# Expert weights of 64 steps copied into a ring of three places, with expert, split buffer and state columns taken from registers

## The chip, the cores and the metric

The kernel runs on one core of one Trainium2 chip. The metric is the device time of one launch in microseconds (us); lower is better.

## The reference

Input x is 16 sequences of 256 rows with 128 channels (4096 rows). It is normalised, and two branches are computed from the normalised rows xn. All data are float32.

```python
xn = layernorm(x)
# branch 1: a gated recurrence over time, per channel
state = state * d_t + u_t ; mixed = r_t * state
s = (groupnorm(mixed) * gn_w + gn_b) * g @ W_out.T + b_out
# branch 2: R = 4 rounds, each over E = 4 experts, top 2 of 4 by a router
cur = xn
for r in range(4):
    logits = cur @ Wg[r] + bg[r]
    cw = softmax over the two largest logits, zero elsewhere
    hmid = gelu(cur @ W1[e] + b1[e])                  # 128 -> 512
    cur = cur + sum_e cw[:, e] * (hmid @ W2[e] + b2[e])   # 512 -> 128
out = x + s * silu(cur)
```

## The kernel before

**Tiling.** The 4096 rows are kept transposed (channels on the partitions) in `cur`, as 8 blocks of 512 columns. A turn is one block in one round, so there are 32 turns; turn k works on block k % 8 in round k // 8. A turn has 4 steps, one for each expert, so there are 128 steps; step s is expert s % 4 of turn s // 4.

**Numbers.** Each fp32 operand is split into a high and a low part of type fp32r, and a product is three matmuls: high by high, low weight by high, high weight by low. The weights of all four experts stay in on-chip memory for the whole kernel, in `w1_hi`, `w1_lo`, `w2_hi`, `w2_lo`. The split of a turn's block is in one of five buffers of `cur_hi` and `cur_lo` (buffer k % 5).

**A step.** `up(s)` on TensorE is 12 matmuls (3 for each of the 4 hidden tiles, lines 1079, 1080, 1083) into `h_bank`. ScalarE applies GELU (L465, output `g`) and makes the high part `g_hi` (L471); VectorE makes the low part `g_lo` (L759). `down(s)` on TensorE is 12 matmuls (L1140, L1142, L1152) into `y_bank`. VectorE combines it with bias and gate into `tmp` (L773, `combine`), and GpSimd issues a DMA that adds `tmp` to the block's columns of `cur` (L415), one in flight at a time. TensorE's order is written out by hand: in iteration s it does `up(s + 1)`, then `down(s)`, then, in some iterations, the router's logits, then in 7 iterations of every 14, beginning at 15, one projection of the recurrent branch (`project`, three matmuls into `p_bank`). `mixers_at` says which: the stage is (s - 15) mod 14, and stages 0, 1, 2, 3, 5, 6 and 12 have a projection, as long as blocks are left.

**Gates.** The router's gates are made for four turns at once. For turns 8 to 11, 12 to 15, 16 to 19 and 20 to 23 VectorE writes them to `cw` (L752) in its iterations 30, 46, 62 and 78. For each turn k, `spread_gates(k)` on SyncE issues a small write of the gates to DRAM (`cw_scratch<-cw`, L312, 8 KB), then waits until it has landed (`cw_saved`), and then issues the read that spreads them over all partitions (`cw_b<-cw_scratch`, L321, 1024 KB). The write waits for `cw_ready` and for `combined` (2 + 4 (k - 1)), which stands for the combine of step 4k - 5. SyncE runs its DMAs in program order, and all its transfers go to one queue (queue 1 of the profile). From turn 4 to 24 SyncE has nothing else to do than `spread_gates`.

**Semaphores that matter here.** `up_done` counts the four hidden tiles of every step, `down_done` the steps whose down is finished, `gelu_done` the GELU tiles, `summed` the landed additions.

Of the kernel before, what the change touches and what calls it, by code (L numbers as in the profile page):

```python
# [5 lines left out]
D = 128  # L6
# [4 lines left out]
BLK = 512  # L11
# [80 lines left out]
def mixer_gated_experts(nc, x, proj_t, mixes, wout_t, chan_vecs, wg, bg, w1, b1, w2, b2, cw_scratch, out):  # L92
# [7 lines left out]
    with ExitStack() as ctx:  # L100
        def sb(name, shape, dt=f32):
            return ctx.enter_context(nc.sbuf_tensor(name, shape, dt))
# [4 lines left out]
        def sem(name):  # L107
            return ctx.enter_context(nc.semaphore(name))
# [3 lines left out]

        cur = sb("cur", [128, TOK])

        w1_hi, w1_lo = sb("w1_hi", [128, E, F], f32r), sb("w1_lo", [128, E, F], f32r)
        w2_hi, w2_lo = sb("w2_hi", [128, E * FT, D], f32r), sb("w2_lo", [128, E * FT, D], f32r)
# [9 lines left out]
        gnw4, gnb2 = sb("gnw4", [128, 1]), sb("gnb2", [128, 1])  # L126
        mix = sb("mix", [128, 6])
        ident = sb("ident", [128, 128])
        warm = sb("warm", [128, 1])

        cur_hi, cur_lo = sb("cur_hi", [128, SPLITS, BLK], f32r), sb("cur_lo", [128, SPLITS, BLK], f32r)
        g = sb("g", [128, 2, FT * BLK])
        g_hi, g_lo = sb("g_hi", [128, 2, FT * BLK], f32r), sb("g_lo", [128, 2, FT * BLK], f32r)
        tmp = sb("tmp", [128, SUMS, BLK])
        cw_b = sb("cw_b", [128, 2, BLK * E])

# [68 lines left out]
        g_lo_done = sem("g_lo_done")  # L205
        down_done = sem("down_done")
        combined = sem("combined")
        r_full, r_empty = sem("r_full"), sem("r_empty")
        p_full, p_empty = sem("p_full"), sem("p_empty")
        lgd_ready, lgth_ready = sem("lgd_ready"), sem("lgth_ready")  # L210
# [15 lines left out]

        def as_f32(ap):
            return ap.bitcast(f32)

        GATEW, SMALL, MIXW = 2, 3, 2  # L230

# [25 lines left out]
        def _(sp):  # L257
# [112 lines left out]
            spread_gates(3)  # L370
            for b in range(4, NB):
                copy_block(b)
            END_TURN = END_FROM // E
            for k in range(4, END_TURN):
                spread_gates(k)
            load_x_again(0)
            load_x_again(1)
# [15 lines left out]
        @block.gpsimd  # L393
        def _(pool):
            pool.memset(ident[:, :], 0.0).then_inc(made, 1)
            pool.memset(ahead[:, :, :, :], 0.0).then_inc(made, 1)
            pool.wait_ge(made, 2)
            pool.affine_select(out=ident[:, :], in_=ident[:, :], compare_op=ALU.not_equal, fill=1.0,
                               base=0, pattern=[[-1, 128]], channel_multiplier=1).then_inc(made, 1)
            pool.memset(cw_e[:, :, :], 0.0).then_inc(gates_padded, 1)  # L400
            pool.memset(xn_t[:, :, 0:1], 0.0).then_inc(edge_zeroed, 1)

            for s in range(STEPS - ADDED_BY_DVE):
                for b in at_step(STORE_BEFORE, s):
# [10 lines left out]
                pool.dma_start(cur[:, block_of(s // E)], tmp[:, s % SUMS, :], accum_op=ALU.add).then_inc(summed, DMA)  # L415

        @block.scalar
        def _(act):
# [8 lines left out]

            def high_w2(e):
                act.wait_ge(w2_loaded[e], DMA)
                nc.scalar.activation(w2_hi[:, e * FT:(e + 1) * FT, :], w2_raw[e], ACT.Copy).then_inc(w2_high, 1)  # L430

            def high_mixw():
                act.wait_ge(mixw_loaded, DMA * MIXW)
# [131 lines left out]
        def _(dve):  # L565
# [71 lines left out]
                                        ALU.subtract).then_inc(w1_low, 1)  # L637

            def low_w2(e):
                h = slice(e * FT, (e + 1) * FT)  # L640
                dve.wait_ge(w2_high, e + 1)
                nc.vector.tensor_tensor(w2_lo[:, h, :], w2_raw[e], as_f32(w2_hi[:, h, :]),
                                        ALU.subtract).then_inc(w2_low, 1)

            def low_mixw():
# [431 lines left out]
        def _(pe):  # L1077
# [4 lines left out]
            def mm_low(out_ap, w_hi, v_lo):  # L1082
                return nc.tensor.matmul(out_ap, w_hi, v_lo, start=False, stop=True)  # L1083

            def turn_normed(b):
# [21 lines left out]
            def up(s1):  # L1107

                k, e = s1 // E, s1 % E
                q = k % SPLITS  # L1110
                if k == 0:
                    pe.wait_ge(w1_low, e + 2 if e > 0 else 1)
                if s1 == 0:
                    pe.wait_ge(first_high, 1)
                if e == 0:
                    pe.wait_ge(cur_split, 2 * k + 1)
                for ft in range(FT):
                    if s1 == 0 and ft == 1:
                        pe.wait_ge(w1_low, 2)
                    if s1 > 0:  # L1120
                        pe.wait_ge(gelu_done, FT * (s1 - 1) + ft + 1)
                    w = slice(ft * D, (ft + 1) * D)
                    mm_high(hb[ft][:, :], w1_hi[:, e, w], w1_lo[:, e, w], cur_hi[:, q, :])
                    if e == 0 and ft == 0:
                        pe.wait_ge(cur_split, 2 * (k + 1))
                    mm_low(hb[ft][:, :], w1_hi[:, e, w], cur_lo[:, q, :]).then_inc(up_done, 1)

            def down(s):

                e, b = s % E, s % 2  # L1130
                if s < E:
                    pe.wait_ge(w2_high, e + 1)
                pe.wait_ge(combined, s + 1)
                if s == 0:
                    pe.wait_ge(p_empty, 1)
                for ft in range(FT):
                    if ft % 2 == 0:
                        pe.wait_ge(g_hi_done, 2 * s + ft // 2 + 1)
                    hi = g_hi[:, b, ft * BLK:(ft + 1) * BLK]
                    nc.tensor.matmul(yb[b][:, :], w2_hi[:, e * FT + ft, :], hi, start=(ft == 0), stop=False)  # L1140
                    if s >= E:
                        nc.tensor.matmul(yb[b][:, :], w2_lo[:, e * FT + ft, :], hi, start=False, stop=False)  # L1142
                if s < E:

                    pe.wait_ge(w2_low, e + 1)
                    for ft in range(FT):
                        nc.tensor.matmul(yb[b][:, :], w2_lo[:, e * FT + ft, :], g_hi[:, b, ft * BLK:(ft + 1) * BLK],
                                         start=False, stop=False)
                for ft in range(FT):
                    if ft % 2 == 0:  # L1150
                        pe.wait_ge(g_lo_done, 2 * s + ft // 2 + 1)
                    last = nc.tensor.matmul(yb[b][:, :], w2_hi[:, e * FT + ft, :], g_lo[:, b, ft * BLK:(ft + 1) * BLK],  # L1152
                                            start=False, stop=(ft == FT - 1))
                last.then_inc(down_done, 1)

            def down_halves(s, sums, done):

                e, b = s % E, s % 2
                pe.wait_ge(combined, s + 1)
                for n in range(2):  # L1160
                    if n == 0 and s == STEPS - 1:
# [3 lines left out]
                    for ft in range(FT):  # L1165
                        if n == 0 and ft % 2 == 0:
                            pe.wait_ge(g_hi_done, 2 * s + ft // 2 + 1)
                        hi = g_hi[:, b, ft * BLK + n * HALF:ft * BLK + (n + 1) * HALF]
                        nc.tensor.matmul(sums[n][:, 0:HALF], w2_hi[:, e * FT + ft, :], hi, start=(ft == 0), stop=False)
                        nc.tensor.matmul(sums[n][:, 0:HALF], w2_lo[:, e * FT + ft, :], hi, start=False, stop=False)  # L1170
                    for ft in range(FT):
                        if n == 0 and ft % 2 == 0:
                            pe.wait_ge(g_lo_done, 2 * s + ft // 2 + 1)
                        lo = g_lo[:, b, ft * BLK + n * HALF:ft * BLK + (n + 1) * HALF]
                        last = nc.tensor.matmul(sums[n][:, 0:HALF], w2_hi[:, e * FT + ft, :], lo, start=False, stop=(ft == FT - 1))
                    last.then_inc(done, 1)

            def logits(n):
# [102 lines left out]
```

## Time and profile before

| what | value |
|---|---|
| time, median of 2 runs (784.88 and 784.97) | 784.92 us |
| span of the profiled execution, first to last instruction | 782.9 us |
| its own time, which is among the two | 784.9 us, 2.0 more than the span |
| TensorE busy | 777.2 us, 99% |
| VectorE busy | 689.3 us, 88% |
| ScalarE busy | 641.1 us, 82% |
| GpSimd busy | 115.2 us, 15% |
| DMA, mean over the span | 81.62 MB, 104 GB/s |
| granted TensorE clock | 1.00 throughout |

The engines are named PE (TensorE matmul), PEld (its weight loads, which run beside the matmuls), DVE (VectorE), ACT (ScalarE), POOL (GpSimd) and SPq (SyncE issuing a DMA). A matmul's row gives the time at which it starts and a modelled length of 0.39 us; back to back they start every 0.23 us. A DMA is issued by an engine's queue, and "to landing" is the time from the start of its issue until its semaphore has been counted up.

### The profile page before, as it was taken

Reading aid. Unit: us, or ns where it says so; the run is one execution under the profiler, and the core shown is the slowest. Engines: PE = TensorE matmul, PEld = TensorE weight load, DVE = VectorE, ACT = ScalarE, POOL = GpSimd, SP = SyncE. Lnnn points to the kernel's source line nnn. Section 1 sums busy time; section 2 is a strip of 40 time slices with the busy share of each in tenths; the row PEclk is TensorE's granted clock in tenths of the full one; section 3 lists DMA queues with packets and bytes.
Section 4 is the critical chain, followed back from the end, with each engine's and each line's share of the span. In section 5 each row is a group of like instructions: output and inputs, shape, how many; then the busy total and the mean of one; then the engine's idle time right before and its main releaser. Section 6 shows DMA issues by size and latency. Waiting matters only on the chain.

```text
span 782.9 us, 9951 instructions
## 1 busy us (share of the span) xinstructions
PE 777.2 (99%) x3392; PEld 619.2 (79%) x3392; DVE 689.3 (88%) x1096; ACT 641.1 (82%) x873; POOL 115.2 (15%) x141
## 2 busy tenths in 40 slices
PE   8999999999999999999999999999999999999998
PEld 6778788887888878888788887888877788888887
DVE  7999987899888889879899788987988989988998
ACT  7989888787888877888788877887877878888886
POOL 0122111111111111111111111111111111111110
PEclk9999999999999999999999999999999999999999
DMA  8467572332642416333154322643227434655453
GB/s 267 139 132 182 128 208 50 95 95 41 148 89 62 107 28 163 92 64 88 33 157 107 81 57 41 149 108 96 41 41 175 108 56 107 134 123 122 70 117 71
DMA packets 77010, 81.62 MB, mean 104 GB/s; under 512 B 48800, under 2 KB 54688, under 8 KB 72992
## 3 DMA queue, kind: packets, MB, share of 16 engines
q0 software_dynamic: 18624, 34.61, 25.8%
q1 hardware_dynamic: 57920, 46.11, 19.5%
q8 instruction: 27, 0.44, 0.2%
q10 hardware_dynamic: 416, 0.26, 0.1%
q14 instruction: 23, 0.19, 0.1%
HBM read 41.91 MB, written 3.93 MB: 59 GB/s over the span
## 4 chain that ended last, share of the span: by engine, by line
PE 95%; ACT 2%; DVE 2%; issue 0%; DMA 0%; DVEq 0%
PE h_bank L1079 15%; PE h_bank L1080 15%; PE h_bank L1083 15%; PE y_bank L1152 15%; PE y_bank L1142 15%; PE y_bank L1140 14%; PE p_bank L1079 2%; PE p_bank L1083 2%; PE p_bank L1080 2%; PE r_bank L1189 1%; ACT g L465 1%; ACT g_hi L471 1%; DVE g_lo L759 0%; DMA cur<-in_x 0%; DVE stats L600 0%
## 5 line engine op out<-in xcount | busy, mean ns | idle before, releaser
L465 ACT ACTIVATE g<-h_bank,b_c 128x512 f32<-128x512 f32 x512 | 329.3, 682 | 77.8 <-PE h_bank L1083 77.0
L759 DVE TENSOR_TENSOR g_lo<-g,g_hi 128x1024 fp32r<-128x1024 f32 x256 | 310.0, 1222 | 72.8 <-ACT g_hi L471 71.2
L471 ACT ACTIVATE g_hi<-g 128x1024 fp32r<-128x1024 f32 x256 | 271.8, 1062 | 8.1
L415 POOL DMA_DIRECT2D cur<-tmp x126 | 110.6, 878 | 642.4 <-DVE tmp L773 544.1
L1079 PE MATMUL h_bank<-cur_hi,w_hi 128*128 128x512 f32 x512 | 202.9, 396 | 0.2 <-ACT cur_hi L513 0.2
L1083 PE MATMUL h_bank<-cur_lo,w_hi 128*128 128x512 f32 x512 | 202.2, 395 | 0.0
L1080 PE MATMUL h_bank<-cur_hi,w_lo 128*128 128x512 f32 x512 | 202.1, 395 | 0.0
L1140 PE MATMUL y_bank<-g_hi,w_hi 128*128 128x512 f32 x504 | 196.2, 393 | 0.0
L1142 PE MATMUL y_bank<-g_hi,w_lo 128*128 128x512 f32 x488 | 193.6, 397 | 0.0
L1152 PE MATMUL y_bank<-g_lo,w_hi 128*128 128x512 f32 x504 | 137.9, 395 | 0.1
L1079 PEld LDWEIGHTS h_bank<-cur_hi,w_hi 128*128 128x128 f32 x512 | 96.2, 188 | 26.6 <-issue 3.8
L1083 PEld LDWEIGHTS h_bank<-cur_lo,w_hi 128*128 128x128 f32 x512 | 96.2, 188 | 23.3 <-DVE cur_lo L663 0.2
L1080 PEld LDWEIGHTS h_bank<-cur_hi,w_lo 128*128 128x128 f32 x512 | 96.3, 188 | 22.6
L1152 PEld LDWEIGHTS y_bank<-g_lo,w_hi 128*128 128x128 f32 x504 | 94.6, 188 | 23.1 <-DVE g_lo L759 0.5
L1140 PEld LDWEIGHTS y_bank<-g_hi,w_hi 128*128 128x128 f32 x504 | 94.7, 188 | 22.4 <-issue 0.8
L1142 PEld LDWEIGHTS y_bank<-g_hi,w_lo 128*128 128x128 f32 x488 | 91.7, 188 | 23.0
L773 DVE SCALAR_TENSOR_TENSOR tmp<-y_bank,b_c,cw_b 128x512 f32<-128x512 f32 x126 | 93.6, 743 | 0.0
L836 DVE SCALAR_TENSOR_TENSOR xm<-xx,mix,xn_t 128x512 f32<-128x512 f32 x48 | 35.7, 744 | 0.3
L824 DVE TENSOR_TENSOR part_lo<-xm,part_hi 128x512 fp32r<-128x512 f32 x48 | 33.2, 692 | 1.7
L708 DVE TENSOR_TENSOR cur_lo<-cur,cur_hi 128x512 fp32r<-128x512 f32 x31 | 21.5, 692 | 1.1
L822 DVE TENSOR_SCALAR part_hi<-xm 128x512 fp32r<-128x512 f32 x48 | 20.8, 434 | 1.6
L1079 PE MATMUL p_bank<-part_hi,pj_hi 128*128 128x512 f32 x48 | 19.3, 401 | 0.0
(153 smaller groups left out, 410.5 us busy)
## 6 DMA issues: line engine op xcount, KB each, us to landing
cur<-tmp POOLq DMA_DIRECT2D x126, 256.0 KB, 3.3
cw_b<-cw_scratch SPq DMA_DIRECT2D x31, 1024.0 KB, 5.2
xn_t<-cur SPq DMA_DIRECT2D x8, 256.0 KB, 3.1
cur<-in_x SPq DMA_DIRECT2D x7, 256.0 KB, 5.0
xr<-in_x SPq DMA_DIRECT2D x28, 64.0 KB, 3.4
out<-o SPq DMA_DIRECT2D x28, 64.0 KB, 2.1
xn_scratch<-o POOLq DMA_DIRECT2D x6, 256.0 KB, 3.0
xr<-xn_scratch SPq DMA_DIRECT2D x24, 64.0 KB, 2.5
```

Of the source, the lines that this page charges most:

```text
L415: pool.dma_start(cur[:, block_of(s // E)], tmp[:, s % SUMS, :], accum_op=ALU.add).then_inc(summed, DMA)
L465: nc.scalar.activation(g[:, gb, ft * BLK:(ft + 1) * BLK], hb[ft][:, :], ACT.Gelu_apprx_tanh, bias=b1_c[:, e * FT + ft:e * FT + ft + 1]).th ...
L471: nc.scalar.activation(g_hi[:, gb, h], g[:, gb, h], ACT.Copy).then_inc(g_hi_done, 1)
L759: nc.vector.tensor_tensor(g_lo[:, gb, h], g[:, gb, h], as_f32(g_hi[:, gb, h]), ALU.subtract).then_inc(g_lo_done, 1)
L773: nc.vector.scalar_tensor_tensor(out=tmp[:, s % SUMS, :], in0=yb[s % 2][:, :], scalar=b2_c[:, e:e + 1], in1=cw_b[:, q, e * BLK:(e + 1) * BLK],
L836: link(nc.vector.scalar_tensor_tensor(out=xm[:, :, :], in0=xx[:, :, :], scalar=mix[:, k:k + 1], in1=xs[:, :, 1:LEN + 1], op0=ALU.mult, op1 ...
L1079: nc.tensor.matmul(out_ap, w_hi, v_hi, start=True, stop=False)
L1080: nc.tensor.matmul(out_ap, w_lo, v_hi, start=False, stop=False)
L1083: return nc.tensor.matmul(out_ap, w_hi, v_lo, start=False, stop=True)
L1140: nc.tensor.matmul(yb[b][:, :], w2_hi[:, e * FT + ft, :], hi, start=(ft == 0), stop=False)
L1142: nc.tensor.matmul(yb[b][:, :], w2_lo[:, e * FT + ft, :], hi, start=False, stop=False)
L1152: last = nc.tensor.matmul(yb[b][:, :], w2_hi[:, e * FT + ft, :], g_lo[:, b, ft * BLK:(ft + 1) * BLK], start=False, stop=(ft == FT - 1))
```

## The change

1. **Ring.** The weights are laid out so that high and low part of one expert are next to each other (`w1_all`, `w2_all`: 2 x 512 elements, 4 KB per partition and expert). A new tile `staged` has three places of 512 KB. For steps 32 to 95 (64 of the 128), TensorE takes its weights from `staged`, not from the resident tiles. SyncE copies them there from on-chip memory: 128 DMAs of 512 KB, one for the up weights and one for the down weights of each step. Units are numbered in the order in which TensorE uses them: up 32, up 33, down 32, up 34, down 33, ... Unit v goes to place v % 3, and from v = 3 on its DMA waits until unit v - 3 has been used (`up_done` or `down_done`).
2. **Waits.** `up(s)` and `down(s)` wait for `stage_full` of their place before their first matmul in these steps.
3. **Order on SyncE.** `stage_step(s)` for the four steps 4(k - 1) to 4k - 1 stands ahead of `spread_gates(k)`. It issues the unit up(s + 1) and the unit down(s) (at s = 32 also up(32)).
4. **Registers.** A table of small numbers is made once by three GpSimd iotas. SyncE loads 4 registers from it (the expert, source of the copy), TensorE 16 registers before `up(24)` (the split buffer of a turn), and GpSimd 16 before its step 24 (the block for the addition). In steps 32 to 95 the 12 moving operands of `up`, the copies and the additions are addressed through them.
5. **Room.** `g_lo` lies in the same bytes as `g`, so that the low part is written over its input.

```diff
+STAGES, STAGED_FROM, STAGED_TO = 3, 32, 96
...
+        w1_all, w2_all = sb("w1_all", [128, E, 2, F], f32r), sb("w2_all", [128, E, 2, F], f32r)
...
+        staged = sb("staged", [128, STAGES, 2, F], f32r)
...
+        g = nc.alloc_sbuf_tensor_at("g", [128, 2, FT * BLK], f32, offset=place)
+        g_lo = nc.alloc_sbuf_tensor_at("g_lo", [128, 2, FT * BLK], f32r, offset=place)
...
+        def unit_of_w1(s):
+            return 0 if s == STAGED_FROM else 2 * (s - STAGED_FROM) - 1
+
+        def unit_of_w2(s):
+            return 2 * (s - STAGED_FROM) + 2 if s < STAGED_TO - 1 else 2 * (s - STAGED_FROM) + 1
...
+            def stage(v, src):
+
+                if v >= STAGES:
+                    u = v - STAGES
+                    n = STAGED_TO - STAGED_FROM
+                    if u == 2 * n - 1:
+                        sp.wait_ge(down_done, STAGED_TO)
+                    elif u == 0 or u % 2 == 1:
+                        sp.wait_ge(up_done, FT * (STAGED_FROM + (u + 1) // 2 + 1))
+                    else:
+                        sp.wait_ge(down_done, STAGED_FROM + (u - 2) // 2 + 1)
+                sp.dma_start(staged[:, v % STAGES, :, :].bitcast(f32), src.bitcast(f32)).then_inc(stage_full[v % STAGES], DMA)
...
+            def stage_step(s):
+
+                if s == STAGED_FROM:
+                    stage(unit_of_w1(s), weights(w1_all, s))
+                if s + 1 < STAGED_TO:
+                    stage(unit_of_w1(s + 1), weights(w1_all, s + 1))
+                stage(unit_of_w2(s), weights(w2_all, s))
+
+            sp.wait_ge(table_made, 3)
+            regs = [sp.alloc_register(f"expert{n}") for n in range(E)]
+            sp.load(regs, table[0:1, 36:40])
...
             for k in range(4, END_TURN):
+                for s in range(E * (k - 1), E * k):
+                    if STAGED_FROM <= s < STAGED_TO:
+                        stage_step(s)
                 spread_gates(k)
...
+                if s1 == STAGED_FROM - 8:
+                    pe.wait_ge(table_made, 3)
+                    regs = [pe.alloc_register(f"slot{n}") for n in range(16)]
+                    pe.load(regs, table[0:1, 3:19])
...
+                if STAGED_FROM <= s1 < STAGED_TO:
+                    at = slots[s1 // E - STAGED_FROM // E]
+                    v_hi, v_lo = (ap[:, bass.ds(at, 1), :].rearrange("p a c -> p (a c)") for ap in (cur_hi, cur_lo))
+                    v = unit_of_w1(s1)
+                    pe.wait_ge(stage_full[v % STAGES], DMA * (v // STAGES + 1))
```

SyncE's order around turns 8, 9 and 10, before the change; each pair of rows is one `spread_gates`:

```order
L321 DMA cw_b<-cw_scratch 128x2048 [waits cw_saved]
L312 DMA cw_scratch<-cw 16x4x32 [waits combined,cw_ready]
L321 DMA cw_b<-cw_scratch 128x2048 [waits cw_saved]
L312 DMA cw_scratch<-cw 16x4x32 [waits combined,cw_ready]
L321 DMA cw_b<-cw_scratch 128x2048 [waits cw_saved]
```

The same engine after the change, from the second half of turn 9's copies over `spread_gates(9)` into turn 10's copies:

```order
L418 DMA staged<-w_all 128x1024 [waits down_done]
L418 REGISTER_ALU [waits up_done]
L418 DMA staged<-w_all 128x1024
L346 DMA cw_scratch<-cw 16x4x32 [waits combined,cw_ready]
L355 DMA cw_b<-cw_scratch 128x2048 [waits cw_saved]
L418 DMA staged<-w_all 128x1024 [waits down_done]
L418 DMA staged<-w_all 128x1024 [waits up_done]
```

Eight copies now stand between two `spread_gates`, and the small write, its wait and the 1024 KB read stand between two copies, in one queue.

TensorE at the start of turn 8 (step 32), before the change: a projection, then the first hidden tiles of `up(32)`:

```order
L1083 MATMUL p_bank<-part_lo,pj_hi 128x512 [waits part_ready]
L1079 MATMUL h_bank<-cur_hi,w_hi 128x512 [waits gelu_done,cur_split]
L1080 MATMUL h_bank<-cur_hi,w_lo 128x512
L1083 MATMUL h_bank<-cur_lo,w_hi 128x512 [waits cur_split]
L1079 MATMUL h_bank<-cur_hi,w_hi 128x512 [waits gelu_done]
```

The same place after the change:

```order
L1160 MATMUL p_bank<-part_lo,pj_hi 128x512 [waits part_ready]
L1156 ISA [waits gelu_done,cur_split,stage_full0]
L1156 MATMUL h_bank<-cur_hi,staged 128x512
L1157 MATMUL h_bank<-cur_hi,staged 128x512
L1160 REGISTER_ALU [waits cur_split]
L1160 MATMUL h_bank<-cur_lo,staged 128x512
L1156 MATMUL h_bank<-cur_hi,staged 128x512 [waits gelu_done]
```

The matmuls are the same; two register instructions per turn and the wait for `stage_full` are added.

## Rows read from the trace of the kernel before

**Rows 1.** The page: busy time by engine.
```profile
PE 777.2 (99%) x3392; PEld 619.2 (79%) x3392; DVE 689.3 (88%) x1096; ACT 641.1 (82%) x873; POOL 115.2 (15%) x141
```
**Rows 2.** The page: the chain that ended last, by engine.
```profile
PE 95%; ACT 2%; DVE 2%; issue 0%; DMA 0%; DVEq 0%
```
**Rows 3.** Timeline of PE around steps 46 to 49: start, length, instruction.
```profile
291.62 0.40 PE L1140 MATMUL y_bank<-g_hi,w_hi 128*128 128x512 f32 x1
...
294.40 0.39 PE L1079 MATMUL p_bank<-part_hi,pj_hi 128*128 128x512 f32 x1
...
295.09 0.39 PE L1079 MATMUL h_bank<-cur_hi,w_hi 128*128 128x512 f32 x1
...
297.89 0.39 PE L1140 MATMUL y_bank<-g_hi,w_hi 128*128 128x512 f32 x1
...
300.69 0.39 PE L1079 MATMUL h_bank<-cur_hi,w_hi 128*128 128x512 f32 x1
```
**Rows 4.** The same timeline: starts of up(32), up(65) and up(81).
```profile
198.11 0.39 PE L1079 MATMUL h_bank<-cur_hi,w_hi 128*128 128x512 f32 x1
...
397.69 0.39 PE L1079 MATMUL h_bank<-cur_hi,w_hi 128*128 128x512 f32 x1
...
493.27 0.39 PE L1079 MATMUL h_bank<-cur_hi,w_hi 128*128 128x512 f32 x1
```
**Rows 5.** Timeline of SPq: spread_gates of turns 8, 12, 16 and 20.
```profile
199.66 0.30 SPq L312 DMA_DIRECT2D cw_scratch<-cw  x1
201.03 0.34 SPq L321 DMA_DIRECT2D cw_b<-cw_scratch  x1
...
296.64 0.30 SPq L312 DMA_DIRECT2D cw_scratch<-cw  x1
298.00 0.34 SPq L321 DMA_DIRECT2D cw_b<-cw_scratch  x1
...
396.62 0.34 SPq L321 DMA_DIRECT2D cw_b<-cw_scratch  x1
...
491.33 0.34 SPq L321 DMA_DIRECT2D cw_b<-cw_scratch  x1
```
**Rows 6.** Timeline of DVE: the gates of turns 12 to 15 are written.
```profile
296.30 0.31 DVE L752 STREAM_TRANSPOSE cw<-cw_e 128x128 f32<-128x128 f32 x1
```
**Rows 7.** DMA issues, 200 to 590 us: count, KB each, median us to landing.
```profile
cw_b<-cw_scratch SPq DMA_DIRECT2D x17, 1024.0 KB, 5.5
cur<-tmp POOLq DMA_DIRECT2D x65, 256.0 KB, 3.3
```
**Rows 8.** The page: DMA issues and the additions' queue (packets, MB, share).
```profile
xn_t<-cur SPq DMA_DIRECT2D x8, 256.0 KB, 3.1
...
q0 software_dynamic: 18624, 34.61, 25.8%
```
**Rows 9.** Stretches: PE, PEld, DVE, ACT, POOL busy, PEclk, DMA share, GB/s.
```profile
200.00:395.00 195.00, 195.00 (x844) 155.32 (x843) 167.70 (x246) 158.04 (x211) 28.36 (x33) 1.00 0.39 87
...
205.00:207.00 2.00, 2.00 (x11) 1.59 (x10) 1.93 (x5) 1.81 (x4) 0.00 (x0) 1.00 1.04 297
```
**Rows 10.** Waits: total us, times, longest.
```profile
SPq L321 <- DMA cw_scratch<-cw: 51.4, 31, 4.5
```
**Rows 11.** Waits of the weight loads with no releaser in sight.
```profile
PEld h_bank L1079 <- issue: 3.8, 5, 0.8
```

More of the change, by code:

```diff
@@ L207, in mixer_gated_experts @@
         combined = sem("combined")
+        table_made = sem("table_made")
+        stage_full = [sem(f"stage_full{q}") for q in range(STAGES)]
         r_full, r_empty = sem("r_full"), sem("r_empty")
@@ L228, in as_f32, with as_f32r, w1_of, w2_of @@
             return ap.bitcast(f32)
+        def as_f32r(ap):
+            return ap.bitcast(f32r)
+        def unit_of_w1(s):
+            return 0 if s == STAGED_FROM else 2 * (s - STAGED_FROM) - 1
+        def unit_of_w2(s):
+            return 2 * (s - STAGED_FROM) + 2 if s < STAGED_TO - 1 else 2 * (s - STAGED_FROM) + 1
+        def w1_of(s):
+            if STAGED_FROM <= s < STAGED_TO:
+                q = unit_of_w1(s) % STAGES
+                return staged[:, q, 0, :], staged[:, q, 1, :]
+            return w1_hi[:, s % E, :], w1_lo[:, s % E, :]
+        def w2_of(s):
+            if STAGED_FROM <= s < STAGED_TO:
+                q = unit_of_w2(s) % STAGES
+                return tuple(staged[:, q, n, :].rearrange("p (t d) -> p t d", d=D) for n in range(2))
+            return w2_hi[:, s % E, :, :], w2_lo[:, s % E, :, :]
         GATEW, SMALL, MIXW = 2, 3, 2
@@ L400, in _ @@
             pool.memset(cw_e[:, :, :], 0.0).then_inc(gates_padded, 1)
+            pool.iota(table[0:1, 0:20], pattern=[[0, 4], [1, SPLITS]], base=0, channel_multiplier=0).then_inc(table_made, 1)
+            pool.iota(table[0:1, 20:36], pattern=[[0, 2], [1, NB]], base=0, channel_multiplier=0).then_inc(table_made, 1)
+            pool.iota(table[0:1, 36:40], pattern=[[1, E]], base=0, channel_multiplier=0).then_inc(table_made, 1)
             pool.memset(xn_t[:, :, 0:1], 0.0).then_inc(edge_zeroed, 1)
+            blocks = None
             for s in range(STEPS - ADDED_BY_DVE):
+                if s == STAGED_FROM - 8:
+                    pool.wait_ge(table_made, 3)
+                    regs = [pool.alloc_register(f"block{n}") for n in range(16)]
+                    pool.load(regs, table[0:1, 20:36])
+                    blocks = [pool.snap(reg, donate=True, min_val=0, max_val=NB - 1) for reg in regs]
                 for b in at_step(STORE_BEFORE, s):
@@ L1139, in down @@
                     hi = g_hi[:, b, ft * BLK:(ft + 1) * BLK]
-                    nc.tensor.matmul(yb[b][:, :], w2_hi[:, e * FT + ft, :], hi, start=(ft == 0), stop=False)
+                    nc.tensor.matmul(yb[b][:, :], w2h[:, ft, :], hi, start=(ft == 0), stop=False)
                     if s >= E:
-                        nc.tensor.matmul(yb[b][:, :], w2_lo[:, e * FT + ft, :], hi, start=False, stop=False)
+                        nc.tensor.matmul(yb[b][:, :], w2l[:, ft, :], hi, start=False, stop=False)
                 if s < E:
@@ L1151, in down @@
                         pe.wait_ge(g_lo_done, 2 * s + ft // 2 + 1)
-                    last = nc.tensor.matmul(yb[b][:, :], w2_hi[:, e * FT + ft, :], g_lo[:, b, ft * BLK:(ft + 1) * BLK],
+                    last = nc.tensor.matmul(yb[b][:, :], w2h[:, ft, :], g_lo[:, b, ft * BLK:(ft + 1) * BLK],
                                             start=False, stop=(ft == FT - 1))
@@ L1158, in down_halves @@
                 e, b = s % E, s % 2
+                w2h, w2l = w2_of(s)
                 pe.wait_ge(combined, s + 1)
@@ L1168, in down_halves @@
                         hi = g_hi[:, b, ft * BLK + n * HALF:ft * BLK + (n + 1) * HALF]
-                        nc.tensor.matmul(sums[n][:, 0:HALF], w2_hi[:, e * FT + ft, :], hi, start=(ft == 0), stop=False)
-                        nc.tensor.matmul(sums[n][:, 0:HALF], w2_lo[:, e * FT + ft, :], hi, start=False, stop=False)
+                        nc.tensor.matmul(sums[n][:, 0:HALF], w2h[:, ft, :], hi, start=(ft == 0), stop=False)
+                        nc.tensor.matmul(sums[n][:, 0:HALF], w2l[:, ft, :], hi, start=False, stop=False)
                     for ft in range(FT):
@@ L1174, in down_halves @@
                         lo = g_lo[:, b, ft * BLK + n * HALF:ft * BLK + (n + 1) * HALF]
-                        last = nc.tensor.matmul(sums[n][:, 0:HALF], w2_hi[:, e * FT + ft, :], lo, start=False, stop=(ft == FT - 1))
+                        last = nc.tensor.matmul(sums[n][:, 0:HALF], w2h[:, ft, :], lo, start=False, stop=(ft == FT - 1))
                     last.then_inc(done, 1)
```

39 lines of the change are left out of this document (28 added, 11 removed).

## The prediction

> **What bounds the kernel now.** I read the page's busy times first. TensorE is busy for 777.2 of 782.9 us and the next engine for 689.3 [rows 1]; the reader should see that nothing but TensorE's stream can set the time. The chain of waits says the same: 95% of the span is PE [rows 2]. The stretch from 200 to 395 us has PE busy for 195.00 of 195.00 us at a granted clock of 1.00 [rows 9]. So there is no hole in the middle to hide anything in: every microsecond for which TensorE waits there is added to the time, and nothing that only gives other engines room takes any away.
>
> Then the timeline of PE gives the beat. An up of 12 matmuls runs from 295.09 to 297.89, a down from there to 300.69: 2.80 us each. A projection between them takes 295.09 - 294.40 = 0.69 us [rows 3]. Last come the DMAs, on which the change lives. SyncE issues a small write, waits for it and then issues the 1024 KB read [rows 5], which lands after 5.5 us; an addition lands after 3.3 us [rows 7]. The DMA engines are taken to 39% [rows 9].
>
> **The change, part by part.**
>
> *What stays.* Matmuls, activations and vector operations keep number, size and order. `g_lo` over `g` needs no new wait, because ScalarE already waits for the down of two steps before when it reuses the buffer. These edits are worth 0.
>
> *One unit alone.* A copy is 512 KB on chip. The nearest row is the on-chip copy of 256 KB, 3.1 us to landing [rows 8]. While the 1024 KB read runs, the engines move 297 GB/s with a share of 1.04 [rows 9], so 512 KB (0.524 MB) are 0.524/0.297 = 1.8 us of data, and 256 KB 0.9. A unit alone lands after 3.1 + 0.9 = 4.0 us. It may be issued when unit v - 3 has been used, and is wanted two phases later, 5.6 us. That covers 4.0 us, and also the data of one addition that meets it, 25.8% of 782.9 us over 126 additions and 6 saves = 1.53 us [rows 8]. Cost 0, with 0.1 us to spare; if the cover goes, each late unit costs its lateness.
>
> *Turns where SyncE is held by the gates.* SyncE takes its work in order. Behind the eight copies of a turn stands `spread_gates(k)`; queued behind its waits are the unit up(4k + 1) and all after it, and TensorE waits for them. At turns 12, 16 and 20 the gates are new. Turn 12 shows it: the up of step 47 ends at 291.62 [rows 3], the gates are written from 296.30 [rows 6], the small write starts at 296.64 and the read at 298.00 [rows 5]. Only then comes the copy for up(49), behind the read's data in the same queue. I let it land 5.5 + 1.8 = 7.3 us after the read's issue: 305.3. TensorE wants it at 300.69 [rows 3], so it waits 4.6 us. Turn 16: 396.62 + 7.3 = 403.9 [rows 5] against 397.69 [rows 4], 6.2 us. Turn 20: 491.33 + 7.3 = 498.6 against 493.27, 5.3 us. Turn 8 is the start of the ring: the first copy stands behind `spread_gates(8)`, whose read starts at 201.03 [rows 5], and up(32) itself needs it, at 198.11 [rows 4]: 201.03 + 7.3 - 198.11 = 10.2 us. Sum of the four: 26.3 us.
>
> *The twelve other turns with a ring behind their gates (9 to 11, 13 to 15, 17 to 19, 21 to 23).* Let T0 be the end of up(4k - 1). Then the last copy of the turn is issued (0.34 us, taken from the read's issue [rows 5]), and the small write behind it. A write costs SyncE 51.4/31 = 1.66 us on average [rows 10], and here it lies behind the copy's 1.8 us of data, of which 0.34 have passed: about 1.4 more. The read is issued at T0 + 0.34 + 1.66 + 1.4 = T0 + 3.4, and up(4k + 1)'s copy lands at T0 + 3.4 + 7.3 = T0 + 10.7. It is wanted after down, up, down: T0 + 8.4, plus 0.69 for each projection after steps 4k - 2 and 4k - 1. By the stage rule three turns have none (10, 13, 17), five have one (11, 14, 18, 19, 21) and four have two (9, 15, 22, 23). Waits of 2.3, 1.6 and 0.9 us: 3 x 2.3 + 5 x 1.6 + 4 x 0.9 = 18.5 us. Turn 24's gates have no copy behind them. After such a wait the next units follow in 1.8 us each and TensorE uses one per 2.8 us, so the ring recovers.
>
> *Bounds of this.* If a copy isn't held by the read's data, it lands 0.34 + 4.0 us after the read's issue: the four waits become 7.3, 1.6, 3.3 and 2.4 = 14.6 us and the twelve none. If additions also meet the units, and the spare 0.1 us is gone by, say, half a microsecond in each of the 48 other staged steps, 24 us come on top. I take the middle, since the read's own share of 1.04 says that the engines have nothing left for a second transfer.
>
> *Registers.* No row shows a register load or a register instruction. TensorE's 16-register load stands once before up(24), and each of 16 turns has two register instructions behind a wait that is long fulfilled. The nearest row is a weight load's idle time with no releaser in sight, longest 0.8 us [rows 11]. From below: nothing, and no gain, as no work goes. From above: 0.8 us for the load and for each of 16 turns, 13.6 us. I take 0.8 for the load and 0 for the pairs, since TensorE's sequencer has the 0.23 us beat of two instructions to run ahead in.
>
> The Trainium skill, "Runtime: NRT & Kernel Launch", section on instruction fetch, gives about 200 ns per register for such a load; by that page TensorE's would be an estimated 3.2 us, and the sum 2.4 us more. No row here shows it.
>
> **Sum.** 26.3 + 18.5 + 0.8 = 45.6 us on the span of 782.9, so 828.5; with the 2.0 us around it 830.5, since the profiled execution's time stands at the median, 784.9. I say 830.
>
> **The rivals.**
>
> *The clock falls in the pauses.* All rows have 1.00, and PE never pauses in them, so for this kernel they show neither level 1.2 GHz nor what brings it. If pauses of 5 to 10 us at turns 8, 12, 16 and 20 bring it, the matmuls behind each run at half speed for a while; a full step of 5.6 us at half speed would lose 5.6, so 0 to 22 us over four pauses. With half a step each: 830 + 11 = 841. For: four pauses longer than any in the trace. Against: no row of a lower clock. The Trainium skill, "TensorE: Matmul & The Clock Gate", in the part on the clock gate, says that an idle TensorE goes to 1.2 GHz and comes back only after sustained work; by that rule this rival comes true.
>
> *The transfer engines become the bound.* Per step they now carry two copies (3.6 us), an addition (1.53) and a quarter of a read (0.9): 6.0 us in a step of 5.6 to 6.3. In shares, 0.39 + 3.6/6.0 = 0.99. If queueing makes half a microsecond per staged step on top, 64 x 0.5 = 32: 862. Against: the 297 GB/s come from a DRAM read; an on-chip copy with 4 KB rows may be quicker.
>
> *Hardly slower.* The copies aren't held by the read, as in the lower bound: 14.6 us and nothing for registers, 799.5, which is not slower beyond 2% of 784.9 (15.7 us, about what a measurement of this kernel can tell from no change). It decides if a copy issued behind the read lands within about 4 us. For: all it needs is that two transfers of one queue overlap. Against: the share of 1.04.
>
> *Register addressing slows TensorE.* 768 matmuls of the staged ups are addressed through a register. If each were late by even 0.05 us, 38 us would come on top: 868. Against: the beat of 0.23 us leaves room.
>
> *The change doesn't do what it says.* The program has the 128 copies and the waits for them, so this needs none of the above: 785, only if all copies hide, and turn 8's can't.
>
> **How the numbers follow.** Forecast 0.45, clock 0.25, engines bound 0.10, hardly slower 0.12, registers 0.05, no effect 0.02, faster 0.01. The range 802 to 866 takes in the bounds of the waits and the clock and leaves out most of the last four. Slower by over 2%: 0.87; within 2%: 0.12; faster: 0.01.
>
> **What would show it.** Right, if the changed kernel's waits have PE waiting for `staged<-w_all`, some 16 times, longest about 10 us at step 32 and 4 to 6 us at three more places; if SPq's rows have up(4k + 1)'s copy right behind `cw_b`, and it lands some 7 us after it; and if the copies elsewhere land in 4 to 5.6 us. The DMA share in the middle should be 0.8 to 1.0. Wrong, if PE waits evenly at all 64 steps (engines bound), if the matmul beat is over 0.23 us without a pause (registers), if a granted clock of 0.5 stands behind the pauses (clock), or if landings behind the read are under 4.5 us (hardly slower).

## The result and the profile after

The changed kernel takes 876.49 us, the median of two runs (871.53 and 881.45), against 784.92 before. The ratio is 1.117, with a 95% interval from 1.102 to 1.132: 92 us slower. The forecast was 830, with a range up to 866. The direction was right, the size was not. The profile is of the run of 871.53, with a span of 869.7. The two runs lie 10 us apart, so a difference of a few microseconds against their median says little.

The page after, for [rows 1] and [rows 2]: busy time by engine, the granted clock in 40 slices, and the chain that ended last.

```profile
PE 795.6 (91%) x3392; PEld 635.6 (73%) x3392; DVE 689.5 (79%) x1096; ACT 639.8 (74%) x873; POOL 115.3 (13%) x144
...
PEclk9999999996999998999989889989999999999999
...
PE 66%; DMA 20%; DVE 7%; ACT 4%; issue 2%; SPq 1%; ACTq 0%; DVEq 0%
```

The reader should see three things. TensorE now has holes (91% against 99%). It is busy for longer (795.6 against 777.2) with the same 3392 matmuls. And the clock line has dips, each at a hole. The other engines do what they did before, in a longer span.

The waits say where the holes are (engine, line, waited for: total us, times, longest):

```profile
PE h_bank L1156 <- DMA staged<-w_all: 67.4, 16, 11.7
PEld h_bank L1156 <- DMA staged<-w_all: 62.2, 15, 7.3
...
PE h_bank L1156 <- issue: 0.6, 1, 0.6
```

TensorE waits for a late copy at 16 places and nowhere else in the 64 steps: at the first matmul of up(32) and of up(4k + 1) for turns 9 to 23, where the forecast put them. The 0.6 us are the load of 16 registers before up(24). In order, the sixteen are 11.7 (turn 8), 2.5, 3.9, 1.9, 6.3 (turn 12), 3.2, 3.6, 1.5, 6.3 (turn 16), 6.1, 3.3, 2.8, 6.8 (turn 20), 2.7, 1.5 and 3.2 us.

The timeline of SyncE's queue at turn 9 shows why. For [rows 5], start, length and DMA:

```profile
228.92 3.29 SPq L418 DMA_DIRECT2D staged<-w_all  x2
232.31 0.58 SPq L346 DMA_DIRECT2D cw_scratch<-cw  x1
236.13 0.34 SPq L355 DMA_DIRECT2D cw_b<-cw_scratch  x1
236.52 2.03 SPq L418 DMA_DIRECT2D staged<-w_all  x2
```

The up of step 35 ends at 231.47. The small write goes out at 232.31, and SyncE waits for it until 236.13. The 1024 KB read goes out then, and the copy for up(37) only behind it, at 236.52. It lands at 243.8, where TensorE's timeline has a wait of 2.53 us.

The pause at step 32 and what follows it, in TensorE's timeline (start, length, idle before):

```profile
208.62 0.79 PE L1156 MATMUL h_bank<-cur_hi,staged 128*128 x1 [11.74 <-DMA staged<-w_all]
209.20 0.63 PE L1157 MATMUL h_bank<-cur_hi,staged 128*128 x1
209.63 0.63 PE L1160 MATMUL h_bank<-cur_lo,staged 128*128 x1
...
217.00 0.39 PE L1156 MATMUL h_bank<-cur_hi,staged 128*128 x1
...
219.76 0.39 PE L1235 MATMUL y_bank<-g_hi,staged 128*128 128x512 f32 x1
...
222.50 0.40 PE L1156 MATMUL p_bank<-part_hi,pj_hi 128*128 128x512 f32 x1
```

The same stretches by the windows (columns as in [rows 9]: busy times, then the granted clock, the DMA share and GB/s), with the one behind the pause of turn 9 at the end:

```profile
197.00:208.60 11.60, 0.00 (x0) 0.00 (x0) 3.71 (x7) 0.51 (x1) 0.91 (x1) 0.61 0.68 189
208.60:212.00 3.40, 3.38 (x8) 2.74 (x9) 0.00 (x0) 1.11 (x2) 0.00 (x0) 0.50 0.51 206
216.00:220.00 4.00, 4.00 (x20) 3.24 (x19) 3.30 (x5) 2.61 (x4) 0.91 (x1) 1.00 0.26 62
243.80:247.00 3.20, 3.20 (x8) 2.55 (x9) 0.54 (x1) 0.96 (x2) 0.56 (x1) 0.51 0.86 302
```

The clock falls from 2.4 to 1.2 GHz within the pause (mean 0.61). Behind it the matmuls start every 0.43 us, not every 0.23, until 213.1. Even 2.5 us of idling at turn 9 have half clock behind them. In this trace half clock stands behind 13 of the 16 pauses, all those of 2.5 us and more, and behind none of the three others (1.9, 1.5 and 1.5 us). At turn 21, with a pause of 2.73 us, it sets in 0.5 us after the first matmul:

```profile
598.40:601.60 3.20, 3.20 (x9) 2.46 (x10) 0.00 (x0) 1.31 (x2) 0.13 (x1) 0.57 0.94 322
```

Last, the beat without pauses: the up from 217.00 to 219.76 takes 2.76 us and the down 2.74, where [rows 3] had 2.80 and 2.80. TensorE is a little faster wherever the clock is full, from the first steps on. No step of the forecast had this.

The DMA issues from 200 to 650 us (count, KB each, median us to landing) answer to [rows 7]:

```profile
staged<-w_all SPq DMA_DIRECT2D x124, 512.0 KB, 3.8
cw_b<-cw_scratch SPq DMA_DIRECT2D x16, 1024.0 KB, 6.5
cur<-tmp POOLq DMA_DIRECT2D x61, 256.0 KB, 3.3
cw_scratch<-cw SPq DMA_DIRECT2D x15, 8.0 KB, 3.0
```

### The profile page after: what moved, and what is told of

Same layout as the page of the kernel before. It is cut to its first block, busy times and chain, and to the rows that moved or that the text cites. A ratio compares the mean times of both kernels' runs of the same rounds, so it can differ in the third digit from the quotient of the medians.

```text
span 869.7 us, 10189 instructions
## 1 busy us (share of the span) xinstructions
PE 795.6 (91%) x3392; PEld 635.6 (73%) x3392; DVE 689.5 (79%) x1096; ACT 639.8 (74%) x873; POOL 115.3 (13%) x144
## 3 DMA queue, kind: packets, MB, share of 16 engines
q1 hardware_dynamic: 76352, 113.23, 39.3%
## 4 chain that ended last, share of the span: by engine, by line
PE 66%; DMA 20%; DVE 7%; ACT 4%; issue 2%; SPq 1%; ACTq 0%; DVEq 0%
DMA staged<-w_all 14%; PE h_bank L1156 12%; PE h_bank L1157 11%; PE h_bank L1160 11%; PE y_bank L1247 9%; PE y_bank L1235 9%; PE y_bank L1237 9%; DMA cw_scratch<-cw 5%; DVE g_lo L836 2%; ACT g L543 2%; ACT g_hi L549 1%; PE p_bank L1156 1%; PE p_bank L1160 1%; PE p_bank L1157 1%; PE r_bank L1285 1%
## 5 line engine op out<-in xcount | busy, mean ns | idle before, releaser
L1156 PE MATMUL h_bank<-cur_hi,staged 128*128 x256 | 112.9, 441 | 67.4 <-DMA staged<-w_all 67.4
L1156 PEld LDWEIGHTS h_bank<-cur_hi,staged 128*128 128x128 f32 x256 | 53.9, 210 | 87.3 <-DMA staged<-w_all 62.2
L1157 PE MATMUL h_bank<-cur_hi,staged 128*128 x256 | 109.8, 429 | 0.0
L1160 PE MATMUL h_bank<-cur_lo,staged 128*128 x256 | 108.7, 425 | 0.0
L1156 PE MATMUL h_bank<-cur_hi,w_all 128*128 128x512 f32 x256 | 101.0, 395 | 0.8 <-issue 0.6
L1235 PE MATMUL y_bank<-g_hi,staged 128*128 128x512 f32 x256 | 100.9, 394 | 0.0
L1237 PE MATMUL y_bank<-g_hi,staged 128*128 128x512 f32 x256 | 100.6, 393 | 0.0
L1157 PE MATMUL h_bank<-cur_hi,w_all 128*128 128x512 f32 x256 | 100.4, 392 | 0.0
L1160 PE MATMUL h_bank<-cur_lo,w_all 128*128 128x512 f32 x256 | 100.0, 391 | 0.0
L1235 PE MATMUL y_bank<-g_hi,w_all 128*128 128x512 f32 x248 | 95.3, 392 | 0.0
L1237 PE MATMUL y_bank<-g_hi,w_all 128*128 128x512 f32 x232 | 90.8, 392 | 0.0
L1247 PE MATMUL y_bank<-g_lo,staged 128*128 128x512 f32 x256 | 69.0, 392 | 0.0
L1247 PE MATMUL y_bank<-g_lo,w_all 128*128 128x512 f32 x248 | 67.0, 392 | 0.4 <-DVE g_lo L836 0.4
L1160 PEld LDWEIGHTS h_bank<-cur_lo,staged 128*128 128x128 f32 x256 | 53.8, 210 | 13.0
L1157 PEld LDWEIGHTS h_bank<-cur_hi,staged 128*128 128x128 f32 x256 | 54.4, 212 | 11.6
L1156 PEld LDWEIGHTS h_bank<-cur_hi,w_all 128*128 128x128 f32 x256 | 48.1, 188 | 14.8 <-issue 3.9
```

The costliest lines, as they stand in the source:

```text
L1156: nc.tensor.matmul(out_ap, w_hi, v_hi, start=True, stop=False)
L1157: nc.tensor.matmul(out_ap, w_lo, v_hi, start=False, stop=False)
L1235: nc.tensor.matmul(yb[b][:, :], w2h[:, ft, :], hi, start=(ft == 0), stop=False)
L1237: nc.tensor.matmul(yb[b][:, :], w2l[:, ft, :], hi, start=False, stop=False)
L1247: last = nc.tensor.matmul(yb[b][:, :], w2h[:, ft, :], g_lo[:, b, ft * BLK:(ft + 1) * BLK], start=False, stop=(ft == FT - 1))
```

## The experiments

Each expectation stands ahead of its result. Times are medians; "before" on the same chips was 784.9 to 785.2 throughout.

| run | us | ratio to before, 95% interval |
|---|---|---|
| changed kernel | 876.49 | 1.102 to 1.132 |
| e1 layout only | 773.87 | 0.984 to 0.988 |
| e3 registers, no ring | 775.07 | 0.986 to 0.989 |
| e2 ring, no registers | 876.09 | 1.113 to 1.122 |
| e4 first copies early | 862.99 | 1.096 to 1.104 |
| e8 small read | 802.42 | 1.021 to 1.029 |
| e14 gates behind copies | 795.02 | 1.010 to 1.015 |
| e7 fill, too long | 888.27 | 1.130 to 1.133 |
| e9 fill, half | 861.27 | 1.095 to 1.102 |
| e5 g over g_lo | 785.07 | 0.999 to 1.001 |
| e6 weights interleaved | 784.85 | 0.999 to 1.001 |
| e10 64 bytes ahead of cur_hi | 785.67 | 1.000 to 1.002 |
| e11 192 bytes ahead of cur_hi | 774.05 | 0.984 to 0.988 |
| e12 64 bytes ahead of the weights | 784.89 | 0.999 to 1.001 |
| e15 only cur_hi and cur_lo moved | 780.83 | 0.992 to 0.996 |
| e16 only the g tiles and those behind | 780.12 | 0.992 to 0.996 |
| e13 all at multiples of 256 | 771.84 | 0.981 to 0.984 |

### Which part costs: layout, registers, ring

**e1, the layout alone.**

```diff
-STAGES, STAGED_FROM, STAGED_TO = 3, 32, 96
+STAGES, STAGED_FROM, STAGED_TO = 3, 1000, 1000
...
```

> The changed kernel without the ring and without registers in the steps (the new layout of the weights, the low part over its input, the idle tile staged and the table stay). In the profile of the changed kernel matmuls start every 0.229 us, before every 0.232, from the first steps on. Theory A (the layout of the tiles makes the beat): 3300 matmuls x 0.0035 = 12 us less than before, 773. Theory B (the beat is the chip's or the run's): the kernel before on the same chip has the same beat, so no difference, 785.

773.87: theory A. The part of the change that moves nothing but places takes 11.1 us off, and the before kernel on the same chip stays at 784.9, so the beat is not the run's. The ring is then dearer than the total shows: against e3 below, which has the layout and the registers but no ring, 876.5 - 775.1 = 101 us.

**e3, registers without the ring.** `w1_of` and `w2_of` give the resident tiles; copies and `stage_full` waits are gone; the matmuls of up and the additions keep their registers.

> Registers in the matmuls of up and in the additions, but no ring: the weights come from the resident tiles. Theory A (registers are free): equal to the layout alone within 2 us. Theory B: up to 38 us more, if each of 768 register-addressed matmuls is late by 0.05 us; a visible hole before up(24) for the load of 16 registers.

775.07, 1.2 us above the layout alone. The one hole is the 0.6 us before up(24). So 768 register-addressed matmuls, 32 register instructions and the load cost together what the forecast gave the load, 0.8, within half a microsecond.

**e2, the ring with fixed addresses.**

```diff
-                return w_all[:, bass.ds(experts[s % E], 1), :, :].rearrange("p a n f -> p (a n) f")
+                return w_all[:, s % E, :, :]
...
```

> The ring as in the change, but all addresses fixed and no register loads. Theory A (registers cost TensorE about nothing): as the changed kernel, 872 to 881, with the same 16 pauses. Theory B (register loads or register addresses cost time on TensorE or delay the copies on SyncE): clearly less, by 10 us or more.

876.09, with waits at the same 16 places (69.2 us). Registers have no part in the loss that these times could show.

### Why the copies are late

**e4, the first three copies ahead of the gates of turn 8.** `stage_step` no longer issues them.

```diff
...
+                if E * k == STAGED_FROM:
+                    stage(unit_of_w1(E * k), weights(w1_all, E * k))
+                    stage(unit_of_w1(E * k + 1), weights(w1_all, E * k + 1))
+                    stage(unit_of_w2(E * k), weights(w2_all, E * k))
                 spread_gates(k)
```

> The changed kernel with the first three copies issued ahead of the gates of turn 8 in place of behind them. Theory A (SyncE, held by the gates, makes the pause of 11.7 us at step 32, and the clock loses some 2 us behind it): that pause goes, 14 us less than the changed kernel, about 862, the other 15 pauses stay. Theory B (the copies are late since the transfer engines are full): the pause shrinks little, over 870.

862.99, 13.5 less. The 11.7 us at step 32 are gone, and 15 waits are left:

```profile
PEld h_bank L1159 <- DMA staged<-w_all: 67.9, 15, 6.9
PE h_bank L1159 <- DMA staged<-w_all: 61.4, 15, 6.5
```

**e8, the read made small.** For turns 8 to 23 the read that spreads the gates takes 64 columns of 2048, so most sums there use stale gates.

```diff
+                if STAGED_FROM // E <= k < STAGED_TO // E:
+                    rest = slice(0, BLK // 8)
```

> The changed kernel, but for turns 8 to 23 the read that spreads the gates takes 64 columns in place of 2048 (32 KB, so that the sums use stale gates there); the small write and the wait for it stay. Theory A (the copy stands behind the read's data in SyncE's queue): copies land some 4 us after the read's issue, not 8 to 9; pauses of about 7 us at step 32 and 2 at turns 12, 16, 17 and 20, nearly none elsewhere; 795 to 805. Theory B (the copies themselves fill the engines): 840 or more.

802.42, as theory A had it, and far under theory B's 840. The same 128 copies move. The profiled run, the longest of five (808.92), has waits of 23.3 us where the changed kernel had 67.4:

```profile
PE h_bank L1158 <- DMA staged<-w_all: 22.3, 7, 8.4
...
PE y_bank L1237 <- DMA staged<-w_all: 1.0, 1, 1.0
```

At turn 8 `up(32)` now starts 5.5 us after the read's issue, with the full read 8.9. First the changed kernel, then e8:

```profile
199.73 0.34 SPq L355 DMA_DIRECT2D cw_b<-cw_scratch  x1
...
208.62 0.79 PE L1156 MATMUL h_bank<-cur_hi,staged 128*128 x1 [11.74 <-DMA staged<-w_all]
```
```profile
200.20 0.34 SPq L357 DMA_DIRECT2D cw_b<-cw_scratch  x1
...
205.70 0.79 PE L1158 MATMUL h_bank<-cur_hi,staged 128*128 x1 [8.35 <-DMA staged<-w_all]
```

The read's data ahead of the copy in the queue cost 3.4 us, about what the missing 0.99 MB (1024 KB less 32) take at 297 GB/s [rows 9], 3.4 to 3.5 us.

**e14, nothing left out, only SyncE's order.** The write of a turn's gates comes behind the first two copies of the next turn, the read behind the third.

```diff
...
+                    for u in units[:early]:
+                        stage(*u)
+                    write_gates(k - 1)
+                    if early == 2:
+                        stage(*units[2])
+                    read_gates(k - 1)
+                    for u in units[3:]:
+                        stage(*u)
...
```

> The changed kernel with SyncE's order changed: the small write of a turn's gates comes behind the first two copies of the next turn and the 1024 KB read behind the third; at turn 8 the first three copies come ahead of both. No work is left out. Theory A (the copies are late since they queue behind the gates): pauses nearly gone, at most about 1 us at 15 places from the read's data, time 778 to 795. Theory B (the engines are full with two copies, an addition and a quarter of a read per step): pauses spread over the steps, 830 or more. Rival C: the gates now come late and VectorE waits, with pauses at combine(4k) of 1 to 4 us each, 800 to 830.

795.02, at the upper edge of what theory A gave. With all its traffic the ring loses 20 us against e3, not 101. The page of this kernel (PE's share, clock, DMA share) and its waits:

```profile
PE 771.9 (97%) x3392; PEld 619.7 (78%) x3392; DVE 689.4 (87%) x1096; ACT 639.3 (81%) x873; POOL 115.6 (15%) x144
...
PEclk9999999999999999999999999999999999999999
DMA  8567573272787778887888778877786436564443
```
```profile
PE y_bank L1255 <- DMA staged<-w_all: 14.8, 12, 3.4
```

The engines are busier than in the changed kernel (7 to 8 tenths, 0.82 from 200 to 390 us), and still all waits at the ups are gone. The waits that are left, 14.8 us at 12 places, are at downs 4k + 1, whose copy stands right behind the read. They are longer than theory A's 1 us (up to 3.4), and TensorE is busy for 5.7 us more than in e3 (771.9 against 766.2). Whether fuller engines lengthen these waits wasn't tested. Rival C shows up at five places, where VectorE waits 0.3 to 1.8 us for the gates; no wait of TensorE is put down to it. So the order in the queue was the cause of 81 of the 101 us, and bandwidth can have a part only in the 20 that are left.

### What the clock costs

**e7 and e9, idle transposes ahead of each late wait.**

`FILLS` gives the number of transposes for each of the 16 steps.

```diff
...
+                    if s1 in FILLS:
+                        pe.wait_ge(r_empty, s1 // 16 + 2)
+                        for _ in range(FILLS[s1]):
+                            nc.tensor.transpose(rb[:, 0:D], ident[:, :], ident[:, :])
```

> The changed kernel with idle transposes (18 to 190 at a place, somewhat shorter than the pause measured there) ahead of each of the 16 waits for a late copy. Theory A (67 us are pauses and the rest of the loss, some 30 us, is matmuls at half clock behind them): granted clock back to 1.00, 774 + 1 + 67 = 842 to 850. Theory B (the matmuls run slow since the copies take memory bandwidth): the time stays at 872 to 881.

888.27, outside both theories: the transposes took 0.11 us each, twice what I had counted, so the fill was longer than the pauses. It tells one thing: the clock was 1.00, and 774 + 1 + 1018 x 0.11 = 887. With full clock and copies in flight the matmuls cost what they cost without, within some 2 us.

> As e7_fill with half as many transposes. In e7_fill they took 0.11 us each, not the 0.055 I had counted, 1018 x 0.11 = 112 us, longer than the pauses; its time is 774 + 1 + 112 = 887. With half of them they end before the copies land. Theory A (half clock behind the pauses is the rest of the loss): clock 1.00, 774 + 1 + 67 = 842 to 850. Theory B (the copies slow the matmuls): 872 or more.

861.27, between the two. The clock stood at 0.996, with half clock left behind two waits (of 2.3 and 2.6 us). From the fill's first transpose to its end in each of the 16 places it took 58 us in all, and TensorE waited for another 21.7:

```profile
PE 829.7 (97%) x3901; PEld 676.2 (79%) x3901; DVE 688.8 (80%) x1096; ACT 639.0 (74%) x873; POOL 115.4 (13%) x144
```
```profile
PE h_bank L1157 <- DMA staged<-w_all: 21.1, 14, 2.9
...
PE y_bank L1240 <- DMA staged<-w_all: 0.6, 1, 0.6
```

The span is 859.2 us, 86.2 more than that of e3. It adds up: 63.5 of longer busy time (829.7 against 766.2; 58 of it are the fill, most of the rest the matmuls at half clock), the 21.7, and one wait of 1.0 for VectorE.

Fill and waits make 80 us where the pauses had been 67. So the clock costs less than the 29 us by which TensorE's busy time exceeds that of the layout alone (795.6 against 766.4): 15 us net by the medians (876.5 - 861.3), 10.5 by the two profiled runs (871.5 - 861.0), and somewhat more if the half clock left in e9 were gone too. The likely reason is that a TensorE at half clock arrives later at the next wait, and some of what it loses it would have spent waiting.

### Where the faster beat comes from

Of the layout's parts, two were tried alone on the kernel before.

> The kernel before, with one part of the layout: g_hi ahead of g, and g_lo in the bytes of g. The layout as a whole took 11.1 us off (784.92 to 773.87). Theory A (the place of g, g_hi and g_lo makes the beat): about 774, matmuls every 0.229 us. Theory B (the weights' layout does): 785 and 0.232.

> The kernel before, with the other part: high and low part of one expert next to each other, nothing else. Theory A (the place of g): 785. Theory B (the weights' layout): about 774, with a beat of 0.229 us.

785.07 and 784.85: neither. Both theories fell, and what was left was where the tiles begin. `staged` (12288 bytes) and the table (192) had moved everything behind them, `cur_hi` from byte 90688, 64 past a multiple of 256, to 103168, a multiple of 256. The diff is e11's, 192 unused bytes; e10 has `[128, 16]` there, 64 bytes.

```diff
+        sb("pad", [128, 48])
         cur_hi, cur_lo = sb("cur_hi", [128, SPLITS, BLK], f32r), sb("cur_lo", [128, SPLITS, BLK], f32r)
```

> The kernel before with an unused 64 bytes per partition ahead of cur_hi. In the kernel before cur_hi begins at byte 90688 (64 past a multiple of 128), in the changed one at 103168 (a multiple of 256). Neither the place of g nor the interleaved weights gave the faster beat. Theory A (a moving operand that begins at a multiple of 128 bytes is read faster): 774, beat 0.229 us. Theory B (it needs a multiple of 256): 785. Theory C (something else in the layout): 785 here and with 192 bytes.

> The same with 192 bytes, so that cur_hi, cur_lo, g_hi and g_lo begin at multiples of 256. Theories A and B: 774, beat 0.229 us. Theory C: 785.

> 64 unused bytes ahead of the weights: they begin at a multiple of 256 (49408, before 49344), and cur_hi at a multiple of 128 (90752). Theory A: 774 from the moving operands; if the weight loads gain too, less than 774. Theory B: 785, or less if only the weights' place matters. Theory C: 785.

With 64 bytes (a multiple of 128) 785.67, with 192 (a multiple of 256) 774.05, with 64 ahead of the weights 784.89. Theory B, for the bytes ahead of `cur_hi`: 256 counts and 128 doesn't. The weights' place alone does nothing.

> The kernel before with 192 bytes ahead of cur_hi and 64 more ahead of g: cur_hi and cur_lo (moving operands of up) begin at multiples of 256, the g tiles and all behind stay 64 past one. If each operand counts by itself, the beat falls in up alone, 1536 matmuls x 0.0035 = 5 us, about 779.5. If only the g tiles or tiles behind them matter: 785.

> The reverse: 192 bytes ahead of g only, so that the g tiles and those behind begin at multiples of 256, and cur_hi and cur_lo 64 past one. If each operand counts by itself, the beat falls in down alone, about 779.5. If all hangs on the g tiles or on what lies behind them: 774.

780.83 and 780.12, 4.4 and 5.1 us off, where both together take 11: each operand counts nearly by itself. e16 also moved the tiles behind the g tiles, but the downs read only g tiles and weights. The phases show it. First e15, then e16 (TensorE's timeline, first matmul of each phase):

```profile
448.29 0.39 PE L1081 MATMUL h_bank<-cur_hi,w_hi 128*128 128x512 f32 x1
...
451.04 0.39 PE L1142 MATMUL y_bank<-g_hi,w_hi 128*128 128x512 f32 x1
...
453.82 0.39 PE L1081 MATMUL p_bank<-part_hi,pj_hi 128*128 128x512 f32 x1
```
```profile
447.47 0.39 PE L1080 MATMUL h_bank<-cur_hi,w_hi 128*128 128x512 f32 x1
...
450.25 0.40 PE L1141 MATMUL y_bank<-g_hi,w_hi 128*128 128x512 f32 x1
...
453.01 0.40 PE L1080 MATMUL p_bank<-part_hi,pj_hi 128*128 128x512 f32 x1
```

In e15 the up, whose moving operands were shifted, takes 2.75 us and the down 2.78; in e16 the up takes 2.78 and the down 2.76.

> The kernel before, with 64 unused bytes ahead of the weights and 128 more ahead of cur_hi: weights, split blocks and g tiles all begin at multiples of 256 bytes. If only the moving operands' place matters: 774, as with 192 bytes ahead of cur_hi. If the weight loads gain from it too: 765 to 772. If what helped was 192 bytes as such and not the multiple of 256 for the tiles behind: 785.

771.84: the fastest of all, 13.4 us under the kernel before (ratio 0.982) and 2 under e11. The weights' place does count a little, once the moving operands are right; the two intervals (0.981 to 0.984 and 0.984 to 0.988) only just part. In its timeline it is the down that gains, 2.72 us:

```profile
446.62 0.39 PE L1142 MATMUL y_bank<-g_hi,w_hi 128*128 128x512 f32 x1
...
449.34 0.40 PE L1081 MATMUL p_bank<-part_hi,pj_hi 128*128 128x512 f32 x1
```

## Why the prediction was wrong

The sum of what was measured closes: 784.9 - 11.1 (layout) + 1.2 (registers) + 67.4 (waits) + 29.2 (TensorE busy longer) = 871.6, against 871.53 of the profiled run. The forecast had 44.8 of waits, 0.8 of registers and nothing for layout and clock. So two of its steps made it too short, and a third hid a part of that: the clock behind the pauses, put at nothing, was 29.2; the waits, with a copy landing too early behind the read, were 22.6 short; and the layout, put at nothing, gave 11.1 back. Point by point:

- **What bounds the kernel.** Right: TensorE alone, and every pause was paid in full.
- **One unit alone hides.** Right, and by more than I thought. The quickest copy landed after 2.9 us, the median after 3.6, where I had 4.0, and no wait stands at the 48 steps where only the ring itself could be late.
- **Turns 8, 12, 16 and 20: 26.3 us.** They took 11.7 + 6.3 + 6.3 + 6.8 = 31.2. The step that failed is the landing "7.3 us after the read's issue": it was 8.7 to 8.9 at all four.
- **The twelve other turns: 18.5 us.** They took 36.2. Of the waits this is the worst-sized term. Two of its pieces were short. The small write, put behind a 512 KB copy, took 3.0 us to land (median), 1.3 before the change; at turn 9 the read went out 4.7 us after T0, not 3.4. And the copy landed 7.2 to 9.2 us behind the read. The read itself had grown from 5.5 to 6.5 us. The landings that I used came from a trace in which the queue was nearly empty.
- **"What stays" is worth 0.** Wrong, by 11 us, and the miss hid part of the other misses. I looked at waits only, not at where the tiles come to lie. e1, e5, e11, e15 and e16 show that the low part over its input is indeed worth 0 and the shift is not.
- **Registers.** Right: 0.8 forecast, 1.2 measured by e3. The Trainium skill, "Runtime: NRT & Kernel Launch", section on instruction fetch, with its 200 ns per register, would by an estimate have made the load 3.2 us; the hole in the trace is 0.6. The page speaks of registers loaded from HBM, and this table lies on chip; the load may also have run partly beside matmuls already issued. The rival with slow register addressing fell with e2 and e3.
- **The clock rival, chance 0.25, 11 us.** It came true. The four long pauses have 46 late starts behind them, 9 us in all, near its 11; what it lacked is that nine shorter pauses had half clock too. Over all the gross loss was 29.2 us, the net one 10 to 15 by e9. This is the dearest term put at nothing: no row of before showed this engine idle for 10 us, so none gave a reason to take the clock behind such a pause at 1.00. The Trainium skill, "TensorE: Matmul & The Clock Gate", in its part on the clock gate, spoke against me, and the trace agrees with it that an idle TensorE falls to 1.2 GHz and comes back only after some work: 0.50 in the window behind the pause of 11.7 us, 1.00 from 216 us on.
- **Engines bound.** Fell with e14: 20 us, with a DMA share of 0.82. The share in the changed kernel was 0.71 from 200 to 650 us, not 0.8 to 1.0. The pauses stretched the steps, and a copy took less than the 1.8 us of its price: q1 is busy for 39.3% of 869.7 us on its page and for 19.5% of 782.9 before, which is an estimated 1.5 us for each of 128 copies if the reads were as before.
- **Hardly slower.** Fell: copies behind the read landed after 7 to 9 us. e8, where the read is small, shows what it would have been.

## What to carry to other kernels

When a new transfer is put into a queue that also carries a write, a wait for it and a big read, price the chain in the new order: what stands behind the wait, and how long each landing is with the new traffic ahead of it. Feeding an engine by prefetch is a matter of order before it is one of bandwidth; here issuing two or three copies ahead of each turn's small write and read took 81 us off. And a pause of some microseconds on TensorE can cost more than its length: its price is the wait plus half-clock matmuls behind it.

Look at where matmul operands begin. Adding or removing a tile shifts all that follow, and this alone was worth 11 us of 785. Try a pad that lets the moving operands begin at a multiple of 256 bytes.

## What the runs showed of the hardware

- A matmul of 128x512 in fp32r starts 0.232 to 0.233 us after the one before if its moving operand begins 64 or 128 bytes past a multiple of 256 in its partition, and 0.229 to 0.230 on average if at a multiple (before, e10, e11, e15, e16). With the weights at multiples too, the downs came every 0.227 us (e13). Other offsets, and other types or widths, weren't tried.
- In the changed kernel the clock was at half behind all 13 pauses of 2.5 to 11.7 us, and not behind three of 1.5 to 1.9 us. Other runs don't part so cleanly: in e2 pauses of 1.8 and 2.0 us had half clock behind them and one of 2.7 had none, and in e4 one of 3.0 had none. What decides there stays open.
- A copy sent behind the read lands later than the read's data explain: in e8 it took 4.9 to 5.2 us from its own issue at turns 8, 12, 16, 17 and 20, against 3.6 for the changed kernel's median copy. At these five turns, and at no others, two more copies are issued within 2.8 us behind it; at the other eleven it took 3.7 to 4.4. The changed kernel has the same five turns apart, 8.3 to 8.8 us against 6.8 to 7.9. This points to the copies sent right behind it, though no run took them away.
